# Local attention: who copies the transposed probabilities of heads 4, 5 and 6 of every eight

## The reference, cut to what matters

```python
def _window_attention(q, k, v, rel_bias):        # per head, |off| <= 32
    def score_step(_, w):
        off = w - HALF
        s = jnp.einsum('bhsd,bhsd->bhs', qh, ks) * scale
        s = s + rel_bias[off + WINDOW][None, :, None]
        s = jnp.where(valid[None, None, :], s, -jnp.inf)
    ...
    attn = jax.nn.softmax(scores, axis=0)
    ...                                           # out = sum over the window of attn * v
h = _layernorm(x, ln_g, ln_b)
lin_out = _linear_attention(h @ wq_lin + bq_lin, h @ wk_lin + bk_lin, h @ wv_lin + bv_lin)
win_out = _window_attention(h @ wq_loc + bq_loc, h @ wk_loc + bk_loc, h @ wv_loc + bv_loc, rel_bias)
gate_in = jnp.concatenate([lin_out, win_out, h], axis=-1)
gate = jax.nn.sigmoid(jnp.maximum(gate_in @ wg1 + bg1, 0.0) @ wg2 + bg2)
out = gate * lin_out + (1.0 - gate) * win_out
return out @ wo + bo + x
```

## Time and profile before

| | |
|---|---|
| median of three runs | 2634.88 us |
| profiled execution | 2637.11 us |
| its span in the trace | 2635.3 us |
| PE busy | 2467.8 us, 94% of the span |
| DVE busy | 1934.5 us, 73% |
| ACT busy | 1616.5 us, 61% |
| POOL busy | 1148.1 us, 44% |

### The profile page before, as it was taken

One profiled execution on the slowest core, in us unless ns is written; L12 is line 12 of the kernel. 1 busy time (PEld: TensorE's weight loads), 2 busy tenths in 40 slices (PEclk: granted clock), 3 DMA queues, 4 the chain that ended last, 5 costly groups with the idle time before them and its releaser, 6 DMA issues. The chain is left out here.

```text
span 2635.3 us, 37625 instructions
## 1 busy us (share of the span) xinstructions
PE 2467.8 (94%) x11094; PEld 1405.0 (53%) x11094; DVE 1934.5 (73%) x3923; ACT 1616.5 (61%) x3503; POOL 1148.1 (44%) x924
## 2 busy tenths in 40 slices
PE   7999989899999999999989999988879998799988
PEld 5767754455555555555444444466644444456655
DVE  7888867799999999999966445466634444577754
ACT  4565533688888888888833344477744443466644
POOL 1000012599999999999930002022200001355442
PEclk8999989999999999999999999999989998999998
DMA  2000024344444444444443221000011110000000
GB/s 110 1 1 1 0 89 94 119 161 161 163 164 159 164 161 164 160 166 157 167 141 82 79 99 65 0 2 1 1 49 65 65 65 28 1 1 1 1 1 17
DMA packets 34771, 205.70 MB, mean 78 GB/s; under 512 B 4016, under 2 KB 5168, under 8 KB 13360
## 3 DMA queue, kind: packets, MB, share of 16 engines
q1 hardware_dynamic: 34608, 203.83, 22.0%
HBM read 201.19 MB, written 2.62 MB: 77 GB/s over the span
## 5 line engine op out<-in xcount | busy, mean ns | idle before, releaser
L1520 POOL TENSOR_TENSOR mam_state_c<-mam_state,weights_r 128x1024 f32<-128x1024 f32 x256 | 600.3, 2365 | 10.1 <-DVE mam_state L1482 8.3
L1482 DVE TENSOR_TENSOR_SCAN mam_state<-banks,mam_dbu 128x1024 f32<-128x1024 f32 x256 | 577.1, 2275 | 1.6 <-ACT banks L1551 0.7
L1601 PE MATMUL banks<-mam_state_c,identity 128*128 128x512 f32 x1024 | 485.0, 606 | 10.6 <-POOL mam_state_c L1520 9.8
L1551 ACT ACTIVATE banks<-mam_dt,mam_a_neg 128x255 f32<-128x255 f32 x1024 | 425.0, 461 | 63.7 <-DVE mam_state L1482 63.2
L1601 PEld LDWEIGHTS banks<-mam_state_c,identity 128*128 128x128 f32 x1024 | 187.2, 190 | 224.1 <-issue 189.2
L1027 PE MATMUL banks<-route_xnt,weights_r 128*128 128x512 f32 x512 | 243.3, 598 | 1.9 <-PEq L736 1.0
L1465 DVE TENSOR_TENSOR mam_dbu<-banks,weights_r 128x1024 f32<-128x1024 f32 x192 | 227.5, 1198 | 0.0
L434 ACT ACTIVATE at_probs<-banks,at_nmax 128x256 f32<-128x256 f32 x256 | 117.9, 473 | 139.1 <-DVE at_nmax L375 139.1
L556 POOL TENSOR_SCALAR route_ln_rs<-route_ln_mv 128x4 f32<-128x4 f32 x16 | 5.1, 318 | 449.3 <-DVE route_ln_mv L634 449.3
L2710 POOL TENSOR_TENSOR at_attention<-at_relu 128x512 f32<-128x512 f32 x128 | 131.2, 1042 | 127.4 <-ACT at_relu L2755 79.7
L975 DVE TENSOR_TENSOR m2b_hidden<-m2b_gelu,m2b_comb_spread 128x512 f32<-128x512 f32 x120 | 80.7, 690 | 116.4 <-ACT m2b_gelu L1005 113.8
(11 more groups left out here) (433 smaller groups left out, 5012.3 us busy)
## 6 DMA issues: line engine op xcount, KB each, us to landing
weights_r<-mam_bc_rows SPq DMA_DIRECT2D x128, 1024.0 KB, 4.7
m2a_comb_spread<-m2a_comb_rows SPq DMA_DIRECT2D x15, 1024.0 KB, 8.0
m2b_comb_spread<-m2b_comb_rows SPq DMA_DIRECT2D x15, 1024.0 KB, 8.0
m1a_comb_spread<-m1a_comb_rows SPq DMA_DIRECT2D x14, 512.0 KB, 6.9
m1b_comb_spread<-m1b_comb_rows SPq DMA_DIRECT2D x14, 512.0 KB, 7.5
weights_r<-in_mb SPq DMA_DIRECT2D x1, 4332.0 KB, 12.9
weights_r<-in_m SPq DMA_DIRECT2D x1, 4200.0 KB, 12.8
weights_r<-in_a SPq DMA_DIRECT2D x1, 2632.0 KB, 10.7
```

The costliest lines, as they stand in the source:

```text
L1482: dve.tensor_tensor_scan(flat2(h[:, i % 4, :, :, :]), decay(i), flat2(dbu[:, i % 4, :, :, :]), 0.0, ALU.mult, ALU.add).then_inc(h_ready, 1)
L1520: pool.tensor_tensor(hc[:, j % 4, :, :, :], h[:, j % 4, :, :, :], c_rows(j), ALU.mult).then_inc(hc_ready, 1)
L1551: i = act.activation(decay(j)[:, o + 1:o + S], dt[:, q, c, 1:S], ACT.Exp, scale=aneg[:, l, k:k + 1])
L1601: k = pe.matmul(y_bank(q)[:, :], K.ident[:, :], flat(hc[:, j % 4, n, :, :]), start=(j == 0 and n == 0), stop=(j == NP - 1 and n == 1))
```

## The change

Before, VectorE copied the transposed probabilities of heads 1, 4 and 6 of every eight (of sixteen: 1, 4, 6, 9, 12, 14). Now it copies those of heads 1 and 5 (1, 5, 9, 13). Heads 4, 6, 12 and 14 go over to ScalarE, heads 5 and 13 to VectorE; 0, 2, 3 and 7 of every eight stay on ScalarE, 1 on VectorE.

```diff
-        BY_DVE = tuple(h for h in range(H) if h % 8 in (1, 4, 6))
+        BY_DVE = tuple(h for h in range(H) if h % 4 == 1)
         BY_ACT = tuple(h for h in range(H) if h not in BY_DVE)
```

## The result

| | kernel before | changed kernel |
|---|---|---|
| median | 2633.15 us (12 runs, 2629.48 to 2635.05) | 2640.91 us (12 runs, 2635.7 to 2645.62) |
| profiled execution | 2637.11 us | 2645.62 us |
| its span | 2635.3 us | 2643.8 us |

The changed kernel is slower: the ratio is 1.0026, interval 1.0018 to 1.0035, which is 7.8 us by the medians and 6.9 by the ratio. The page of its profile says that work only changed hands: TensorE is busy for 2462.5 us (before 2467.8), VectorE for 1925.8 (1934.5) and ScalarE for 1622.9 (1616.5).

A forecast was written before the change was run, and what follows sets the result against it. TensorE was taken as the bound, waiting mostly for ScalarE. Terms of 3.4 + 2.8 + 1.4 + 0 + 1.8 gave 9.4 us slower, 2634.9 + 9.4 = 2644.3 us, range 2637 to 2653 (forecast's own 2641 to 2648, chance 0.70).

The forecast's parts named there:

- The price of a copy, 0.48 us: On ScalarE without idle time, each added copy delays what follows it by 0.48 us.
- Head 6, 0.48 seven times: Slot 8, sequences 0 to 6: the copy delays L1778 and TensorE's L1797 by 0.48 us each time, 3.4 us together.
- Head 4, 0.39: Slot 6: L2197 waits for L2055, 0.39 us in sequences 1 to 6 and 0.48 in the last, 2.8 us together.
- Heads 12, 13 and 14, 0.23: Edge between sequences: 0.23 us left into sequences 1, 2, 4 and 6, 0.48 in the last; together 1.4 us.
- The loop's returns, 0: Returns into sequences 3 and 5: gain and loss on VectorE cancel, 0 us; bounds +0.7 to -4.7 each.
- The last sequence, 1.8: Head 9's maxima wait goes, net -0.25; head 13's copy delays L666 and L582 by 2.06; together 1.8 us, bounds 0 to 3.
- A: Rival: TensorE, idler in each sequence, has its granted clock fall; four clean sequences falling gives 2655 us; chance 0.11.
- B: Rival: VectorE's shorter loop (254 instructions, not 261) loses its stop at both returns, -4.7 us each, 2634.8 us; chance 0.19, whole or part.
- the rule in the prediction: VectorE's loop: blocks of 256 instructions, two held, refilled ahead in sequence; a taken branch stalls if its target isn't held.

The follow-up runs named there:

- forty memsets: Forty one-column memsets of a spare tile on VectorE ahead of the attention loop, added to the kernel before (2621.71 us) and to the changed kernel (2631.01 us).
- L2079 first: Changed kernel with ScalarE's eviction L2079 made ahead of its copy of head 4's probabilities in slot 6; 2635.31 us in one run.
- changed, 8 memsets: Changed kernel with eight one-column memsets of a spare tile on VectorE ahead of the attention loop; 2641.25 us (6 runs).
- changed, 9 memsets: Changed kernel with nine one-column memsets of a spare tile on VectorE ahead of the attention loop; 2652.48 us in one run.
- fourteen heads by ScalarE, 14 memsets: Changed kernel with VectorE copying heads 1 and 9 alone, ScalarE the other fourteen, and fourteen memsets ahead of VectorE's loop; 2635.96 us in one run.
- four of eight by VectorE, 40 memsets: Kernel before with forty memsets, VectorE copying heads 1, 4, 5, 6 of eight, router's combine weights ahead of head 13's copy; 2621.57 us, ratio 0.9953.
- single groups of heads: Kernel before with one pair moved: heads 4, 12 to ScalarE 2637.51 us; heads 6, 14 to ScalarE 2632.64; heads 5, 13 to VectorE 2640.10.

## Why the prediction was right

It forecast 9.4 us more than before and there are 7.8; the time of 2644.3 is 3.4 above the measured 2640.9, of which 1.7 comes from the median of three runs that it started from (2634.88; that of twelve is 2633.15). The direction and the places are right. How near the sum came is in part luck, as its terms by place show. Measured is one profiled execution against one, and the same pair with forty memsets each, which have no stops:

| place | forecast | measured | with forty memsets |
|---|---|---|---|
| sequence 0 | 0.5 | -1.3 | 0.8 |
| sequences 1, 2, 4 and 6 | 4.4 | 3.3 | 4.2 |
| sequences 3 and 5, at the returns | 1.7 | -0.6 | 2.1 |
| sequence 7 and behind it | 2.8 | 3.9 | 3.4 |
| the stage | 9.4 | 5.3 | 10.4 |

In the profiled pair 3.2 of 8.5 us lie outside the stage, where nothing was changed. Step by step:

**The price of a copy, 0.48 us.** Right: behind the copies of heads 4 and 6 the next work of ScalarE starts 0.48 and 0.47 after them.

**Head 6, 0.48 seven times.** The size was nearly right (the third group is 7.33 instead of 6.89 or 6.90: 0.43 to 0.44; alone 0.39). The wait that was named came as forecast (0.98 against about 0.9). But that it costs because L1778 stands behind the copy was only half of it: with L1778 ahead of it the cost stayed, since the value product waits for the end of the same queue.

**Head 4, 0.39.** Right: L2197's wait is 0.36, the group 0.35 longer (8.71 against 8.36), and the last of the three things behind it is what counts. In the last sequence the wait went from 0.89 to 1.38, 0.49 for the forecast 0.48.

**Heads 12, 13 and 14, 0.23.** Near: heads 12 and 14 cost 0.48 and 0.17 alone, head 13 gives 0.24 back. Odd sequences against odd ones with forty memsets are 0.26 longer in the first and last groups (6.59 + 6.47 against 6.82 + 5.98), even ones 0.18. Against the even sequence of before, which the prediction read, nothing is left of it, since the 0.2 us that this form had in its last group are gone: that is the main reason why a clean sequence takes 29.03 and not the forecast 29.4. How the wait is shared out was wrong: L2180's was to go from 0.39 to 0.87 and went to 0.46. L2150 waits 0.34 and not 0.23, and a wait of 0.41 for ScalarE's copy has come ahead of the transposes between the two.

**The loop's returns, 0.** In waiting this held. What is late next is indeed the product behind head 1's maxima, and VectorE's first maxima come 2.83 us behind the first scores instead of 2.61. TensorE's wait for head 14's copy was to go, though, and stays with 1.82, since on ScalarE that copy stands behind head 0's exponential and so behind the first stop. The sequences at the returns have 2.28 and 2.30 us more waiting than a clean one of before with forty memsets (5.11 and 5.13 against 2.83), in the changed kernel 2.17 and 2.13 more than theirs (6.21 and 6.17 against 4.04). Yet in length the returns got cheaper: they are 4.97 and 5.05 us over a clean sequence without stops (28.06) before, and 3.8 and 3.6 over theirs (29.09) after. Of these 2.6 us in two returns 2.4 are TensorE's busy time, at a clock of 0.95 instead of 0.90. That the change raised the clock isn't shown: the two returns with L2079 first have the changed kernel's stops and differ by 2.0 us between 1.00 and 0.90. The prediction's bounds (+0.7 to -4.7 for each) hold it.

**The last sequence, 1.8.** The copy ahead of L666 was right (2.21 for 2.06 + 0.24), and the wait for head 9's maxima is gone, which gives 0.36 for the forecast 0.25. The clock was left out of the sum and only in its bounds: TensorE's busy time is 1.9 us longer from the last sequence's start to the next stage, less of it ahead of L582 and more behind. The profiled execution has 3.9 there for 2.8 (with head 4's 0.48 and the edge's 0.48), and 3.4 with forty memsets.

**Rivals.** A did not happen: clean sequences keep 1.00 with waits of 0.34 to 0.98. B did not happen, and the reason against it that the prediction gave, that a return as such seems to cost the stop, is wrong: forty instructions ahead of the loop took both stops away. A loop seven instructions shorter did nothing; where the loop lies did. And 254 was the wrong number to hold against a piece's size, since it leaves out the waits. The loop's instructions, counted from 0 in the order of VectorE's program with the waits on semaphores, and its returns:

| kernel | first to last | at a return | packets of q14 |
|---|---|---|---|
| before | 2844 to 3139 | two stops, the second at 2852 | 98 |
| changed | 2842 to 3130 | two stops, the second at 2852 | 98 |
| changed, 8 memsets | 2850 to 3138 | two, the second at 2852, seen as one of 4.9 us | 98 |
| changed, 9 memsets | 2851 to 3139 | two, the second at 2852, seen as one of 4.8 to 5.0 us | 98 |
| fourteen heads by ScalarE, 14 memsets | 2852 to 3134 | none | 88 |
| changed, 40 memsets | 2882 to 3170 | none | 88 |
| before, 40 memsets | 2884 to 3179 | none | 88 |
| four of eight by VectorE, 40 memsets | 2888 to 3189 | none | 88 |

The three kernels with single groups of heads stop at 2852 too, 12, 10 and 4 instructions behind their heads. So the edge is known to the instruction: a loop whose head lies one ahead of it stops at each return, and one whose head lies on it doesn't.

The Trainium skill, Runtime: NRT & Kernel Launch, section Instruction fetch mechanics, says that a taken branch stalls when its target isn't among what is held. The runs agree: the stops come with packets of instructions, and without packets there are none. It gives blocks of 256 instructions; the packets here are of 8.2 KB, half of such a block at the 16 KiB that it gives for one. By blocks of that size the next edge would lie at 3108, an estimate that no run measures. The loops that stop would then lie in three blocks and those that don't in two, which fits the two that are held by the rule in the prediction. What stays open: whether a loop that starts behind the edge stops when it is long enough to reach a third block, and whether one that starts ahead of 2852 and ends ahead of 3108 doesn't. It was also not tried whether the same edge can be met by moving the loop back.

## What to carry to other kernels

Price a piece of work that changes its engine at the wait of the bounding engine, not by how busy the two engines are: VectorE did the copies of heads 4, 6 and 12 at no visible cost in a clean sequence, ScalarE needs 0.34 to 0.48 us of the sequence for each. Such a piece costs most of its pitch in the queue (0.4 of 0.48 us) even if what stands directly behind it is moved ahead, as long as the end of the queue is waited for. And when an engine shows idle time put down to "issue" right behind a branch back, look at the instruction queues' packets: if they run during the stop, shifting the loop by some instructions may take away all of it (a head ten instructions later than the changed kernel's was enough here), which with forty memsets was worth more than the change itself (11 us against 8). Count the waits on semaphores too when you look for the edge.

## What I had not expected of the hardware

- VectorE's two stops at a return (2.69 and 1.24 us in the changed kernel, 2.99 and 1.51 before) come with packets of its code, three within 6 us of the return and five a pass; a loop of 296 or 302 instructions can also return with none, and the same work then takes 28.06 instead of 33.03 us. The second stop stands at one instruction of the program, 2852, in all ten kernels that stop.
- The same two stops don't cost the same each time: in one execution the sequence at one return took 31.43 us at a granted clock of 1.00, at the other 33.44 at 0.90.
- In the profiled execution of the changed kernel a wait of 2.21 us ahead of the serial tail went with a granted clock of 0.58 over the 21 us behind it. Another kernel with the same wait had 0.91, and one with a wait of 0.92 had 0.58, so that the wait alone doesn't decide it.
